# Attention loop: the distance terms as one contraction of 96 rows over stacked copies, eight queries of eight heads a product; row maxima in the score banks

## What is computed

```python
emb = box_relational_embedding(boxes)          # [b, n, m, 8]: sin and cos of 100 * log distances
g = relu(einsum('bnmd,hd->bhnm', emb, Wg) + bg)                        # 16 heads
q, k, v = heads(queries @ Wq.T + bq), heads(keys @ Wk.T + bk), heads(values @ Wv.T + bv)   # 16 x 64
a = einsum('bhqd,bhkd->bhqk', q, k) / 8
mn = softmax(log(clip(g, 1e-6)) + a, axis=-1)
out = einsum('bhqk,bhkd->bqhd', mn, v).reshape(b, nq, 1024) @ Wo.T + bo
# mixture of experts, per expert e: acc + (silu(x @ gate_e) * (x @ up_e)) @ down_e * coeff_e, plus a shared expert
```

## Time and profile before

| | us |
|---|---|
| runs | 567.46, 569.45, 567.07 |
| median | 567.46 |
| profiled execution, time | 567.08 |
| profiled execution, span of the core's instructions | 565.3 |
| attention loop, about | 50 to 332 of the span |
| TensorE busy in the span | 456.3 (81%) |
| VectorE, ScalarE, GpSimd busy | 422.6, 379.4, 231.8 |

### The profile page before, as it was taken

The page is one execution under the profiler, slowest core; times in us unless marked ns, Lnnn a source line. Parts: engine busy times, 40 slices in busy tenths (PEclk is TensorE's granted clock), DMA queues, the critical chain, the costliest instruction groups (busy, mean ns, idle before and its releaser), DMA issues. The chain is left out here.

```text
span 565.3 us, 15054 instructions
## 1 busy us (share of the span) xinstructions
PE 456.3 (81%) x5672; PEld 341.9 (60%) x5685; DVE 422.6 (75%) x1001; ACT 379.4 (67%) x704; POOL 231.8 (41%) x215
## 2 busy tenths in 40 slices
PE   6256789999999999999999966454597805999996
PEld 6245678888888888888888752143254403466664
DVE  7976768788887787778788749885388787766664
ACT  4575577887888878887886537865487715755543
POOL 3630443233242342433233214013699930366554
PEclk9659999999999999999999986575555555999999
DMA  8303300000000000000000006004100000000000
GB/s 217 88 0 83 84 2 2 3 3 0 0 0 0 0 2 3 0 0 0 0 0 2 1 3 100 13 2 98 29 2 2 3 0 1 1 1 20 20 14 26
DMA packets 19239, 11.67 MB, mean 21 GB/s; under 512 B 10064, under 2 KB 17128, under 8 KB 19192
## 3 DMA queue, kind: packets, MB, share of 16 engines
q1 hardware_dynamic: 18220, 10.07, 7.9%
q0 software_dynamic: 384, 0.60, 0.5%
q10 hardware_dynamic: 588, 0.36, 0.2%
HBM read 6.64 MB, written 1.05 MB: 14 GB/s over the span
## 5 line engine op out<-in xcount | busy, mean ns | idle before, releaser
L824 POOL TENSOR_TENSOR gprob<-gprob 128x512 f16<-128x512 f32 x64 | 74.8, 1168 | 139.6 <-ACT gprob L1038 139.4
L1134 DVE SCALAR_TENSOR_TENSOR gprob<-psG,prob 128x512 f32<-128x512 f32 x64 | 44.0, 687 | 19.7 <-ACT prob L1072 13.3
L1038 ACT CAST gprob<-gprob 128x512 f16<-128x512 f32 x64 | 39.6, 619 | 23.8 <-DVE gprob L1134 23.8
L903 PEld LDWEIGHTS psG<-kron,emb 128*128 128x128 f16 x768 | 48.8, 99 | 9.2
L903 PE MATMUL psG<-kron,emb 128*128 128x128 f16 x768 | 53.9, 220 | 0.0
L1127 DVE TENSOR_REDUCE negmax<-psM 128x4 bf16<-128x512 f32 x64 | 43.6, 682 | 11.5 <-PE psM L881 11.5
L2112 POOL TENSOR_TENSOR inter<-inter 128x512 f16<-128x512 f32 x32 | 37.0, 1158 | 25.8 <-ACT inter L2163 25.8
L1072 ACT ACTIVATE prob<-psS 128x512 f32<-128x512 f32 x64 | 34.6, 592 | 12.9 <-PE psS L895 12.8
L891 PE MATMUL psS<-qT,kT 64*128 64x128 f32 x512 | 37.2, 284 | 5.7 <-ACT qT L1020 4.0
L1020 ACT ACTIVATE qT<-aux,biasT 128x128 f32<-128x128 f32 x128 | 36.5, 368 | 7.2 <-PE aux L859 7.2
L2156 ACT ACTIVATE act_g<-psEG 128x512 f32<-128x512 f32 x32 | 19.1, 597 | 31.3 <-PE psEU L2273 30.9
(11 more groups left out here) (362 smaller groups left out, 1190.2 us busy)
## 6 DMA issues: line engine op xcount, KB each, us to landing
kS<-ctxT SPq DMA_DIRECT2D x24, 64.0 KB, 2.3
out_dram<-x_sb SPq DMA_DIRECT2D x4, 256.0 KB, 2.3
qS<-qT SPq DMA_DIRECT2D x12, 64.0 KB, 3.0
raw<-in_L_xattn_Wq_dram SPq DMA_DIRECT2D x1, 512.0 KB, 9.5
raw<-in_L_xattn_Wk_dram SPq DMA_DIRECT2D x1, 512.0 KB, 7.4
raw<-in_L_xattn_Wv_dram SPq DMA_DIRECT2D x1, 512.0 KB, 8.1
raw<-in_L_xattn_Wo_dram SPq DMA_DIRECT2D x1, 512.0 KB, 7.5
w<-in_L_ffn_w_dram SPq DMA_DIRECT2D x2, 256.0 KB, 2.9
```

Source lines behind the costliest of these rows:

```text
L824: nc.gpsimd.tensor_tensor(gprob2[:, u % 2, 1], gprob[:, u % 2], gprob2[:, u % 2, 0], ALU.subtract).then_inc(gplo_ready, 1)
L903: mm = mm_(psG[:, :, GN * g:GN * g + GN], emb2[:, par, e_part, g], unit(kron2[:, w_part], u), start=False, stop=(g == NG - 1 and e_part == ...
L1038: nc.scalar.copy(gprob2[:, u % 2, 0], gprob[:, u % 2]).then_inc(gphi_ready, 1)
L1134: v.scalar_tensor_tensor(out=flat(gprob[:, u % 2]), in0=flat(psG[:]), scalar=1e-6 * G_UP, in1=flat(prob[:, u % 2]), op0=ALU.max, op1=ALU.m ...
```

## The change

The contraction of the distance term is 96 rows in place of 128, three times 32: a row is one of four kinds times one of eight queries (N8 = 8, GX = 4, NX = 16). SyncE copies the high part of the embedding twice and the low part once into `embS` (32 partitions each, 128 KB a transfer, 3 transfers a batch), and `kronS` holds high, low, high factors of eight heads in its 96 rows. A product then makes eight queries of eight heads, 64 columns; sixteen of them and four `spin` products of 256 columns make both units of a pair, into a `psG` of two banks. To free that bank, `maxima` write into the score banks `psS`, so they wait until both exponentials of the pair before are done. `psG` is in the order query, head, so scores and their maxima terms are written with `queries` (one f32 in four) and the value products read their weights that way; queries are permuted, which the turning of x before the loop and `att_turn` set right by products with a permuted identity. In the last batch the output projection is in two parts in its own bank `psO`. The load of later weights comes after the transfers of batch 1. In the experts' phase VectorE makes the low part of the last two chunks, and the last shared down product is moved behind chunk 29's. Cut to its core:

```diff
-        kron2=sb("kron2", [P, 2, H0, GN], F16, scope),
+        kronS=sb("kronS", [P, UN, N8, HG], F16, scope),
+        embS=sb("embS", [P, 2, GX, NG, P], F16, scope),
...
-                    mm = nc.tensor.transpose(psT[:, n % 3, j], block_in, ident[:])
+                    if 8 <= n < 12:
+                        mm = nc.tensor.matmul(psT[:, n % 3, j].rearrange("p (g x n) -> p g x n", g=NG, x=GX), block_in,
+                                              ident[:].rearrange("p (g n x) -> p g x n", g=NG, x=GX), start=True,
+                                              stop=True)
...
-    psG, psV = bank("psG"), bank("psV")
-    psM = [bank("psM0"), bank("psM1")]
+    psG = scope.enter_context(nc.psum_tensor("psG", [P, NX, 2, N8, HG], F32))
+    psV, psO = bank("psV"), bank("psO")
...
+    def queries(a, j):
+
+        return flat(a).rearrange("p (m j) -> p m j", j=HG)[:, :, j]
+
+    def stacked(b, par):
+
+        return 3 * 8 * (b - par) + 3 * 16
...
+            def stack(g, par):
+                after(sp, emb_hi, g)
+                after(sp, geo_psum, 2 * (g - 1))
+                for part in range(2):
+                    sp.dma_start(embS[GN * part:GN * part + GN, par], emb2[:, par, 0]).then_inc(emb_in[par], 16)
+                after(sp, emb_lo_odd if par else emb_lo_even, g + par)
+                sp.dma_start(embS[2 * GN:3 * GN, par], emb2[:, par, 1]).then_inc(emb_in[par], 16)
...
+            for g in range(B):
+                stack(g, g % 2)
+                if g == 1:
+                    load_weights()
...
-                        mm = mm_(psM[odd][:, j], upper(qT[rows_of(h), par, h // 2]),
+                        mm = mm_(psS[odd][:, j], upper(qT[rows_of(h), par, h // 2]),
...
-                        mm_(psS[odd][:, j], kT[rows_of(h), par, h // 2], qT[rows_of(h), par, h // 2],
+                        mm_(queries(psS[odd], j), kT[rows_of(h), par, h // 2],
+                            qT[rows_of(h), par, h // 2],
...
-                        mm = mm_(psS[odd][:, j], negmax[:, odd, j:j + 1].to_broadcast([P, P]), identb[:],
+                        mm = mm_(queries(psS[odd], j), negmax[:, odd, j:j + 1].to_broadcast([P, P]),
+                                 identb[:],
...
-            def geometry(b, par, half, u):
-                mm_(psG[:], spin[:, b], unit(spun[:, half], u), start=True, stop=False, skip_group_check=True)
-                for g in range(NG):
-                    for e_part, w_part in ((0, 0), (0, 1), (1, 0)):
-                        mm = mm_(psG[:, :, GN * g:GN * g + GN], emb2[:, par, e_part, g],
-                                 unit(kron2[:, w_part], u), start=False,
-                                 stop=(g == NG - 1 and e_part == 1), skip_group_check=True)
+            def geometry(b, par, half, pair):
+                for k in range(2):
+                    qs = slice(NX // 2 * k, NX // 2 * k + NX // 2)
+                    for odd in range(2):
+                        u = 2 * pair + odd
+                        mm_(psG[:, qs, odd].rearrange("p q n j -> p j q n"), spin[:, b],
+                            spun[:, half, HG * u:HG * u + HG].rearrange("p j (q n) -> p j q n", n=N8)[:, :, qs],
+                            start=(odd == 0), stop=False, skip_group_check=True)
+                for q in range(NX):
+                    mm = mm_(psG[:, q], embS[0:3 * GN, par, q % GX, q // GX], kronS[0:3 * GN, 2 * pair:2 * pair + 2],
+                             start=False, stop=(q % (NX // 2) == NX // 2 - 1), skip_group_check=True)
                 mm.then_inc(geo_psum, 1)
...
-                        mm = mm_(v[:, j * (DK + 1):(j + 1) * (DK + 1)], gprob2[:, u % 2, p_part, j],
+                        mm = mm_(v[:, j * (DK + 1):(j + 1) * (DK + 1)], queries(gprob2[:, u % 2, p_part], j),
...
-                    mm = nc.tensor.transpose(aux[into][:, j], att[:, par, 2 * c:2 * c + 2], ident[:])
+                    mm = mm_(aux[into][:, j].rearrange("p (g n x) -> p g n x", g=NG, x=GX),
+                             att[:, par, 2 * c:2 * c + 2].rearrange("p h e -> p (h e)"),
+                             ident[:].rearrange("p (g x n) -> p g n x", g=NG, x=GX), start=True, stop=True)
...
                 scores(par, 0)
-                maxima(par, 1)
-                after(pe, emb_lo_odd if par else emb_lo_even, b + 1 if par else b)
+                pe.wait_ge(emb_in[par], stacked(b, par))
                 after(pe, gprob_ready, UN * b)
                 geometry(b, par, half, 0)
...
                 v_proj(b, 1, 1)
-                pe.wait_ge(gprob_ready, UN * b + 1)
-                geometry(b, par, half, 1)
+                pe.wait_ge(prob_ready, UN * b + 2)
+                maxima(par, 1)
...
-                geometry(b, par, half, 2)
+                geometry(b, par, half, 1)
...
+                    pe.wait_ge(prob_ready, UN * b + 4)
                     maxima(nxt, 0)
-                pe.wait_ge(gprob_ready, UN * b + 3)
-                geometry(b, par, half, 3)
...
-            for u in (2, 3):
-                wait_pv(B - 1, u)
-                pv((B - 1) % 2, u)
+            pe.wait_ge(att_ready, UN * (B - 1) + 2)
+            att_turn((B - 1) % 2, 0, 1)
+            wait_pv(B - 1, 2)
+            pv((B - 1) % 2, 2)
+            pe.wait_ge(attT_ready, 2 * B - 1)
+            out_part(psO, range(0, CH // 2))
+            wait_pv(B - 1, 3)
+            pv((B - 1) % 2, 3)
...
-                after(act, geo_psum, UN * (g - 1))
+                after(act, emb_in[par], stacked(g - 2, par))
                 nc.scalar.copy(emb2[:, par, 0], wave[:, par]).then_inc(emb_hi, 1)
...
+            dve.wait_ge(lo_ready, EC * NT - 2)
+            for n in (EC * NT - 2, EC * NT - 1):
+                dve.wait_ge(hi_ready, n + 1)
+                v.tensor_tensor(inter2[:, n % RING, 1], inter[:, n % RING], inter2[:, n % RING, 0],
+                                ALU.subtract).then_inc(lo_ready, 1)
...
             for n in range(EC * NT - LAG, EC * NT):
+                if n == EC * NT - 2:
+                    shared_down(NT - 1)
                 routed_down(n)
```

148 lines of the change are left out of this document (87 added, 61 removed).

## The result

The changed kernel takes 624.85 us (median of 4 runs, 624.75 to 625.75) against 567.27 us for the kernel before: 1.101 times as long, 95% interval 1.098 to 1.104. The span of its profiled execution is 623.0 us in place of 565.3. Of the 57.7 us more, the first scores of the loop come 3.6 us later (59.4 against 55.9), the loop from there to the last scores takes 318.5 us in place of 265.5, the last batches some 2.3 us more, and the experts' phase gives back 1.2 us, as forecast.

The account below looks back on a forecast made before the run. TensorE was the bound by busy time, but VectorE and ScalarE were taken to close most stretches of the loop. 567.1 + 11.5 (loop) + 0.5 (before it) - 1.2 (experts) = 577.9 us; range 553 to 592, likeliest sign 571 to 585.

Parts of the forecast that it names:

- The turning: Transposing the attention output in the loop: two f32 passes a block, eight passes 1.03 us, 0.40 more each, 0.80 a batch.
- Strided outputs: Scores, maxima terms and position term written to PSUM one f32 in four: no row gave a price, none was added.
- distance product: TensorE's distance terms for two units: 0.45 us plus 0.48 us, together 0.93 in place of 1.80, saving 1.74 a batch.
- Rival A: TensorE in the loop: strided outputs cost double, +4.1 us a batch of work, +42 us in all, 609 us; chance 10%.
- Three of four stretches would stay as long with a shorter TensorE: Loop, between marked VectorE weighings (probabilities times distance terms): TensorE is full, yet shortening it would leave three of four unchanged.
- even first to third: From first to third VectorE weighing of an even batch, 7.67 us, set by VectorE's queue: +0.7 us for the later reductions.
- even third to odd first: From an even batch's third weighing to the next odd batch's first, 9.36 us, closed by ScalarE: +0.1 us.
- odd first to third: From first to third weighing of an odd batch, 7.61 us: +0.6 us, or +0.1 with the transposing step no longer than before.
- odd third to even first: From an odd batch's third weighing to the even batch's first: new 128 KB transfer makes TensorE wait 0.8 us, +0.25 us.
- "+0.1" for the normalising behind both weighings: VectorE's first normalisation stands behind third and fourth weighing of a batch; query evacuation at +3.9 instead of +3.80 us.
- Before the loop, +0.5: Ahead of the loop: sixteen transposings of x go from one pass to two, 0.1 us each, most beside evacuations: +0.5 us.
- The experts: Experts' phase: last shared down product moved to where TensorE waits, VectorE makes the last low half: together -1.2 us.

Follow-up runs that it names:

- the kernel of single steps: A separate kernel without attention, measuring single products and VectorE/ScalarE instructions with contiguous and strided operands; contiguous f16 product of 128 columns 0.056 us.

## Why the prediction was wrong

The steps that failed are prices of TensorE's products. The turning was put at 1.03 us and took 1.88; strided outputs were put at no cost, and cost 0.42 us in the position products and 0.38 in the maxima terms, each twice a batch. With all operands in order, and the turning back to one pass, the time fell from 624.85 to 576.45 us, which covers the miss of 47 us.

*The turning.* "0.13 each, so eight passes are 1.03" took its price from passes that read contiguously. With its moving operand permuted it took 1.88 us. This is the largest miss, 0.85 us twice a batch, and no rival contained it: I asked what the output's stride costs, not the input's. Putting it right gave 22.6 us of loop, and the second pass less 4.8 more. The "0.40 more" for the second pass was low too: it was set against 0.63 us, which holds the drain. By starts a transposed turning is 0.57 us, and two passes in order are 0.99 to 1.07.

*Strided outputs.* "No row of before has such an output, so the trace gives no price and the sum takes none" is the second step that failed. Of the 0.93 us for the distance product the sixteen products were right (0.48, measured 0.50). The position products, 0.45 "at one column rate", took 0.87 us because they write one f32 in four; in order they take 0.48. Rival A had this mechanism, at double for everything, 609 us. It is real for f16 and bf16 products (0.84 for 0.46 us in the maxima terms) and not for f32 passes, so the scores, the larger part of its 42 us, did not pay. (Its sum is 0.1 us low: 16.4 + 4.1 - 0.94 is 19.5 or 19.6.)

*VectorE's stretches.* "Three of four stretches would stay as long with a shorter TensorE" failed for work added: 13.6 us on the kernel before cost 10.7 in the loop, where 3.5 was forecast. For work taken away nobody tried it on the kernel before. With all in order TensorE is busy 25.9 us less and the loop is longer, which fits the sentence, but shared banks and transfers were added there too. That TensorE and VectorE's chain are nearly equal in this loop, and the one that gets more leads, would explain both; it is argued, not shown.

*The terms of the rest.* They can be read where all operands are in order. The time was 576.45; the forecast's terms with a one-pass turning give 574.4, and 35.15 us the pair, measured 35.3. Term by term it fits less well: even first to third +0.1 in place of +0.7; even third to odd first +0.16 in place of +0.1; odd first to third 0 in place of +0.1; odd third to even first +1.04 in place of +0.25. In the last the transfer made TensorE wait 1.29 us, not 0.8, since 128 KB took 3.2 us to land where I took 2.6. The shared banks by themselves cost 0.8 us a pair and 5.1 us of loop, not 1.2 and 8. That the sum came out some 2 us off is partly chance. And the forecast's own design, two passes in order, was never run: by what the second pass cost elsewhere, 4.7 us in the changed kernel and 12.4 in the kernel before, it would stand at an estimated 581 to 589 us, the upper part of it beyond the forecast's 571 to 585.

*"+0.1" for the normalising behind both weighings.* Too small once TensorE was relieved: with it put back between them the pair fell from 34.3 to 33.9, and TensorE's wait for it had been 1.0 to 1.2 us a batch.

*Before the loop, +0.5.* It was 3.6. The first projection comes 2.6 us later: sixteen more passes of the turning of x cost 0.23 us each and not 0.1, and the position factors take 32 products, each reading in strides, in place of 16. The other 1.0 us is the projections at the lower clock. *The experts* were right.

## What to carry over

Cost each operand of a product by the step in which it is read or written, all three of them, and not by a row of the same count and type; a permutation that one instruction gets for nothing by an access pattern is paid on TensorE for every column, and was free where VectorE or ScalarE read PSUM. When a design misses, measure its steps alone first: here the layout was 48 of the 58 us, and the order of work made up the rest. Compare the pair that repeats before the total: the first pair and the start carried the clock, which changed from one kernel's trace to the next, and hid a gain of 1.0 us a pair. With 25.9 us less of TensorE's work this loop was still the longer one until the order of work was made for it; and an instruction moved up on one engine moves what GpSimd and VectorE do at the same time.

## What the runs showed of the hardware

- A 128-column f16 product takes 0.056 us; with its output not contiguous 0.108 at a step of 8 or 16 bytes, in runs of eight f32 nothing more. Reading in steps of 4 bytes costs nothing, 8 bytes double. An f32 pass (0.112) costs no more with its output one f32 in four or its moving operand in steps of 8 bytes; steps of 16 bytes double it. At the lower clock a pass is 0.22 in order and 0.23 with steps of 16 bytes.
- Weights one f16 in four: the value product 0.40 us in place of 0.36.
- ScalarE writing memory one f32 in four: 0.88 us in place of 0.48; reading PSUM in steps of 128 f32, 0.49.
- A VectorE instruction of 0.34 us took up to 1.30 beside GpSimd.
- A wait of 2 to 3 us on TensorE can bring the granted clock from 1.00 to 0.50 for the next 4 us, in some executions of the same work and not in others. What decides it stays open. The clock also fell without any wait: in the kernel of single steps, with TensorE never idle, it went from 1.00 to 0.50 at 44 us, among products that read one f16 in eight, stayed there through those that read one in sixteen, and was back at 1.00 by 58 us, among contiguous f32 passes.
